# Slot attention with a top-1 switch layer: the second group's outputs finished by slot and scattered to their tokens

## The reference, cut to what matters

```python
x = x + slot_attention(layernorm(x), ctx_1024, ...)          # three GRU steps
t = layernorm(x)
logits = t @ Wg                                               # (4, 512, 8)
gates  = softmax(logits);  expert = argmax(gates)
gate   = gates[expert];    pos = cumsum(onehot(expert)) - 1   # place within the expert
keep   = pos < 64                                             # capacity of an expert, per batch
expert_inputs[e, pos] = t                                     # the kept tokens
y = gelu(expert_inputs @ W1[e]) @ W2[e]                       # (8 experts, 64 slots, 128)
x = x + gate * y[expert, pos]                                 # a dropped token keeps x
```

## Time and profile before

| What | us |
|---|---|
| median of 3 timed runs | 147.28 |
| the profiled execution, its own time | 144.78 |
| its span, first to last instruction | 143.0 |
| so outside the span | 1.8 |
| mean granted TensorE clock in the span | 0.994 |

### The profile page before, as it was taken

The page is one execution under the profiler, slowest core; times in us unless marked ns, Lnnn a source line. Parts: engine busy times, 40 slices in busy tenths (PEclk is TensorE's granted clock), DMA queues, the critical chain, the costliest instruction groups (busy, mean ns, idle before and its releaser), DMA issues.

```text
span 143.0 us, 2755 instructions
## 1 busy us (share of the span) xinstructions
PE 125.9 (88%) x1030; PEld 89.9 (63%) x1030; DVE 95.2 (67%) x305; ACT 80.7 (56%) x156; POOL 33.8 (24%) x54
## 2 busy tenths in 40 slices
PE   6847789999899899899896898699999999889960
PEld 2443466575484575575563764399999899678730
DVE  2895992399699797896998899975781050043851
ACT  1746572586566747847825958963693273044440
POOL 5580922200500501403200052015000187600000
PEclk9999999999999999999999999999999999999997
DMA  3989980000000000000000000000102111102024
GB/s 102 293 221 342 387 298 14 0 0 0 7 0 0 0 0 5 0 2 0 0 5 0 0 0 0 0 5 0 39 5 70 40 37 43 34 5 76 9 66 147
DMA packets 9197, 8.05 MB, mean 56 GB/s; under 512 B 601, under 2 KB 7028, under 8 KB 9184
## 3 DMA queue, kind: packets, MB, share of 16 engines
q1 hardware_dynamic: 8492, 7.28, 15.9%
q0 software_dynamic: 256, 0.40, 1.1%
q10 hardware_dynamic: 436, 0.20, 0.5%
HBM read 6.43 MB, written 1.57 MB: 56 GB/s over the span
## 4 chain that ended last, share of the span: by engine, by line
PE 64%; DVE 16%; ACT 10%; issue 3%; DMA 3%; POOL 2%; ACTq 0%; DVEq 0%
PE ps L1301 11%; PE ps L1287 10%; PE ps L1106 7%; PE ps L1099 6%; PE ps L1133 6%; PE ps L1125 5%; ACT r_b L421 4%; PE ps L1313 3%; PE ps L1207 3%; DMA x_tok<-in_x_dram 3%; PE ps L1170 2%; DVE xn_tok L622 2%; PE ps L1055 2%; PE ps L1082 2%; DVE ps L710 2%
## 5 line engine op out<-in xcount | busy, mean ns | idle before, releaser
L1287 PE MATMUL ps<-h,W_t 128*128 128x128 f32 x128 | 15.9, 279 | 0.0
L1133 PE MATMUL ps<-attn,VW 32*128 32x256 f32 x144 | 12.9, 426 | 3.3 <-DVE ps L710 2.4
L428 ACT ACTIVATE ps<-ps,half_b 128x512 f32<-128x512 f32 x12 | 7.9, 662 | 13.6 <-PE ps L1106 13.6
L1287 PEld LDWEIGHTS ps<-h,W_t 128*128 128x128 f32 x128 | 15.0, 192 | 0.5 <-issue 0.3
L1125 PE MATMUL ps<-h,whhT 128*128 128x256 f32 x48 | 13.5, 403 | 0.0
L1106 PE MATMUL ps<-h,whhT 128*128 128x256 f32 x48 | 13.3, 398 | 0.0
L710 DVE SCALAR_TENSOR_TENSOR ps<-r_b,ps 128x512 f32<-128x512 f32 x12 | 7.8, 693 | 7.7 <-ACT r_b L421 7.7
L345 POOL DMA_INDIRECT y_tok<-y_rows,row_of x8 | 8.5, 1057 | 17.1 <-DMA y_rows<-y_sb 15.0
L1133 PEld LDWEIGHTS ps<-attn,VW 32*128 32x128 f32 x144 | 5.7, 182 | 10.2 <-DVE ps L710 4.8
L1099 PE MATMUL ps<-h,whhT 128*128 128x256 f32 x48 | 11.8, 384 | 0.0
L318 POOL TENSOR_SCALAR mse<-attn 128x8 f32<-128x8 f32 x6 | 1.2, 204 | 44.0 <-DVE attn L645 44.0
(11 more groups left out here) (168 smaller groups left out, 259.5 us busy)
## 6 DMA issues: line engine op xcount, KB each, us to landing
W_t<-in_L_ffn_W_dram SPq DMA_DIRECT2D x1, 2048.0 KB, 10.8
x_tok<-in_x_dram SPq DMA_DIRECT2D x4, 256.0 KB, 4.0
out_dram<-h SPq DMA_DIRECT2D x4, 256.0 KB, 2.3
y_rows<-y_sb SPq DMA_DIRECT2D x4, 128.0 KB, 1.8
n_b<-in_L_xattn_gru_whh_dram SPq DMA_DIRECT2D x1, 192.0 KB, 3.8
n_b<-in_L_xattn_gru_wih_dram SPq DMA_DIRECT2D x1, 192.0 KB, 3.1
y_tok<-y_rows,row_of POOLq DMA_INDIRECT x8
n_b<-in_ctx_dram ACTq DMA_DIRECT2D x1, 64.0 KB, 3.3
```

The lines of the kernel that those rows point to most:

```text
L428: nc.scalar.activation(HV[i], HV[i], ACT.Identity, bias=half_b[:, 2:3]).then_inc(s["hb"], 1)
L1133: last = mm(to[:, hf, :], VW[b][p:p + M, gate * P:(gate + 1) * P], attn[g][p:p + M, :], start=False, stop=True, skip_group_check=True)
L1287: last = mm(hid_bank[e][:, j * BG * CAP:(j + 1) * BG * CAP], W1_t[:, ex_, j * P:(j + 1) * P], rhs, start=True, stop=True)
```

## The change

For group 1 the whole return by matmul goes (`slot_rows`, `rows_out`, `combine_hot`, `y_high`, `y_low`, `combine`, the copies of the sums, `back`, `gated_out`). In its place:

- x of group 1 is kept in `x2_row`, 128 channels, then the gate, then the token's number in `out`: rows of 130 words. SP stores the 128 channels to `out` early, so that dropped tokens are done.
- SP fills an HBM tensor `slot_rows` (1024 rows of 130 words) with a "no token" mark, and POOL writes each token's row to its slot there, 8 indirect DMAs (`file_tokens`), ahead of the 8 fetches of group 0. SP reads it back in slot order (`slot_row`), one DMA a batch.
- Each half of a `down` of group 1 is finished by one DVE instruction (gate times y plus x, `finished_rows`) and written by one indirect DMA of POOL to its tokens in `out` (`send_rows`, 8 of them); rows without a token are out of bounds.
- So the gate of group 1 is needed early: `scale_logits(1)` stands ahead of `place(1)`, `gates(1)` behind it, and `gate_exp(1)` on ACT behind `gelu(1)`, as Tanh with (1 + t) / (1 - t) on DVE instead of Exp. On PE `logits(2)` and `logits(3)` stand ahead of `up(1)`, `positions(1)` ahead of `down(0)`.
- Batch 3's halves of group 1's `down` go to banks 4 and 5. `source_rows` of group 0 move behind the dispatch of group 1.
- PE's preamble has `keep_clock(2)` and `keep_clock(5)` more.

```diff
+            sp.wait_ge(marks, 3)
+            sp.dma_start(slot_rows.ap().rearrange("(k p) d -> p k d", p=P),
+                         no_token[:, :].unsqueeze(1).broadcast_to([P, BG * NP, ROW])).then_inc(cleared, 16)
+            for b in range(BG, B):
+                sp.wait_ge(x2c, b + 1)
+                sp.dma_start(out[b].rearrange("(c p) d -> p c d", p=P),
+                             x2_row[:, (b - BG) * C:(b - BG + 1) * C, 0:D]).then_inc(kept_out, 16)
             for k in range(NP):
                 sp.wait_ge(ysb, k + 1)
                 sp.dma_start(y_rows..., y_sb[:, k, :, :]).then_inc(y_put, 16)
-            for b in range(B):
-                sp.wait_ge(fin, (C, 2 * C, 3 * C, 3 * C + 1)[b])
+            for i in range(BG):
+                sp.wait_ge(tok_put[i], 16 * C)
+                sp.dma_start(slot_row[:, :, i, :], slot_rows...[i]).then_inc(slot_got[i], 16)
+            for b in range(BG):
+                sp.wait_ge(fin, (b + 1) * C)
                 sp.dma_start(out[b]..., res[:, b, :]...).then_inc(out_done, 16)
...
+            def file_tokens(b):
+                for n in range(b * C, (b + 1) * C):
+                    nc.gpsimd.indirect_dma_start(
+                        out=slot_rows.ap(), out_offset=bass.IndirectOffsetOnAxis(ap=row_of[:, n:n + 1], axis=0),
+                        in_=x2_row[:, n - CG, :], in_offset=None,
+                        bounds_check=BG * E * CAP - 1, oob_is_err=False).then_inc(tok_put[b - BG], 16)
+            def send_rows(s, i):
+                k = s - NP
+                pool.wait_ge(rs, BG * k + i + 1)
+                nc.gpsimd.indirect_dma_start(
+                    out=out.rearrange("b n d -> (b n) d"),
+                    out_offset=bass.IndirectOffsetOnAxis(ap=slot_row[:, k, i, TOKEN_AT:ROW].bitcast(u32), axis=0),
+                    in_=y_sb[:, k, i, :], in_offset=None,
+                    bounds_check=B * N - 1, oob_is_err=False).then_inc(rows_out_done, 16)
+            pool.wait_ge(cleared, 16)
+            pool.wait_ge(x2c, B)
+            pool.wait_ge(gt, 2)
+            pool.wait_ge(idx, BG)
+            file_tokens(2)
+            file_tokens(3)
             pool.wait_ge(y_zero, 1)
-            pool.wait_ge(idx, BG)
+            pool.wait_ge(idx, B)
             pool.wait_ge(y_put, 16 * NP)
             fetch_rows(0)
             fetch_rows(1)
+            pool.wait_ge(kept_out, 16 * BG)
+            for s in range(NP, STEPS):
+                send_rows(s, 0)
+                send_rows(s, 1)
...
             gelu(1)
+            gate_exp(1)
             y_out(0)
...
             x2_shift(3)
+            scale_logits(1)
             place(1)
+            source_rows(2)
+            source_rows(3)
+            gates(1)
             dispatch_hot(2)
             x_low(2)
             dispatch_hot(3)
             x_low(3)
+            source_rows(0)
+            source_rows(1)
+            dve.wait_ge(y_put, 16 * NP)
             dve.wait_ge(gt, 1)
+            finished_rows(NP, 0)
+            finished_rows(NP, 1)
             gated_rows(0)
+            finished_rows(NP + 1, 0)
+            finished_rows(NP + 1, 1)
             gated_rows(1)
+            for s in range(NP + 2, STEPS):
+                finished_rows(s, 0)
+                finished_rows(s, 1)
...
             up(0)
             x2_back(3)
-            up(1)
             logits(2)
             logits(3)
+            up(1)
+            positions(1)
             down(0)
-            positions(1)
             up(2)
...
-            slot_rows(2)
-            slot_rows(3)
             pe.wait_ge(xeC, B)
             up(4)
             up(5)
             down(4)
             up(6)
             down(5)
-            combine(4)
             up(7)
             down(6)
-            combine(5)
             down(7)
-            combine(6)
-            combine(7)
-            back(2)
-            back(3)
```

More of the change, by code:

```diff
@@ L463, in gate_exp @@
                 act.wait_ge(gl, g + 1)
-                nc.scalar.activation(lex[:, cs, :], lg[:, cs, :], ACT.Exp).then_inc(lx, 1)
+                if g == 0:
+                    nc.scalar.activation(lex[:, cs, :], lg[:, cs, :], ACT.Exp).then_inc(lx, 1)
+                else:
+                    nc.scalar.activation(lex[:, cs, :], lg[:, cs, :], ACT.Tanh, scale=0.5).then_inc(lx, 1)
             def dispatched_out(b):
@@ L577, in _ @@
             dispatched_out(3)
-            rows_out(2)
-            rows_out(3)
-            gelu(4)
             for s in range(NP, STEPS):
[L582 to L593, removed]
+                gelu(s)
         @block.vector
@@ L829, in gates @@
                 dve.wait_ge(lx, g + 1)
+                if g == 1:
+                    v.tensor_scalar(first[:, cs, :], lex[:, cs, :], -1.0, 1.0, ALU.mult, ALU.add).then_inc(sg, 1)
+                    dve.wait_ge(sg, 1)
+                    v.reciprocal(first[:, cs, :], first[:, cs, :]).then_inc(sg, 1)
+                    dve.wait_ge(sg, 2)
+                    v.scalar_tensor_tensor(out=lex[:, cs, :], in0=lex[:, cs, :], scalar=1.0, in1=first[:, cs, :],
+                                           op0=ALU.add, op1=ALU.mult).then_inc(sg, 1)
+                    dve.wait_ge(sg, 3)
                 v.reduce_sum(lsum[:, cs], lex[:, cs, :], AX).then_inc(ls, 1)
                 dve.wait_ge(ls, g + 1)
-                v.reciprocal(gate[:, cs], lsum[:, cs]).then_inc(gt, 1)
+                v.reciprocal(gate[:, cs] if g == 0 else x2_row[:, :, GATE_AT], lsum[:, cs]).then_inc(gt, 1)
             half_biases()
@@ L895, in _, with source_rows @@
             gates(0)
[L897 to L917, removed]
-                v.tensor_scalar(row_of[:, cs], slot[:, cs], float(i * E * CAP), None, ALU.add).then_inc(idx, 1)
+            def source_rows(b):
+                cs = slice(b * C, (b + 1) * C)
+                dve.wait_ge(pl, 5 * (b // BG + 1))
+                v.tensor_scalar(row_of[:, cs], slot[:, cs], float((b % BG) * E * CAP), None, ALU.add).then_inc(idx, 1)
             def gated_rows(b):
@@ L1017, in _ @@
             tr(bank[0][:, P:2 * P], Wv_t[:, :], ident[:, :]).then_inc(wtr, 1)
+            keep_clock(2)
             pe.wait_ge(m_c, 2)
@@ L1030, in _ @@
             mm(bank[3][:, 256:256 + E], center[:, :], Wg_t[:, :], start=True, stop=True).then_inc(m_p, 1)
+            keep_clock(5)
             norm_T(1)
@@ L1183, in positions @@
                 mm(to, tri[:, :], of, start=False, stop=True, skip_group_check=True).then_inc(posP, 1)
-            def slot_rows(b):
-                g = b // BG
-                pe.wait_ge(pl, 6 * g + 6)
-                pe.wait_ge(x2c, BG)
-                for c in range(C):
-                    last = mm(row_bank[b % BG][:, c * P:(c + 1) * P],
-                              slot_r[:, b * C + c:b * C + c + 1].broadcast_to([P, P]),
-                              ident_r[:, :], start=True, stop=True)
-                last.then_inc(srP, 1)
             def dispatch(b):
@@ L1298, in down @@
                 for i in range(BG):
+                    to = y2_bank if s >= NP and i == 1 else y_bank
                     for j in range(J):
                         for e in range(2):
[L1301 removed]
+                            last = mm(to[s % 2][e * CAP:(e + 1) * CAP, i * D:(i + 1) * D],
                                       hid[s % 2][:, e, j, i * CAP:(i + 1) * CAP], W2_t[:, 2 * k + e, j, :],
                                       start=(j == 0), stop=(j == J - 1))
[L1304 to L1328 removed]
+                    if s >= NP:
+                        last.then_inc(yB, 1)
+                if s < NP:
+                    last.then_inc(yP, 1)
             pe.wait_ge(w1_in, 16)
```

141 lines of the change are left out of this document (48 added, 93 removed).

## The result

The changed kernel takes 148.43 us (median of 6 runs, 147.66 to 149.44), the kernel before 145.45 (6 runs, three of them those of the section above). The ratio is 1.024, interval 1.019 to 1.029: slower. Forecast were 141.6 and the range 138.5 to 145.0. Its profiled execution has a span of 147.7 us where I had 137.3.

What follows compares the result with a forecast made beforehand. PE's chain was taken to bound the kernel before, POOL's queue the changed one: last send 134.04 + 2.3 landing + 0.4 = 136.7, plus 0.6 unplaced waits, 137.3 span; profiled 139.1, median 141.6, range 138.5 to 145.0.

Steps and rivals of the forecast that it cites:

- POOL's queue: POOL's file_tokens, fetches and sends in sequence; claimed to set the end, 2.9 us behind what PE allows.
- a scatter's pitch: Time from one scatter on POOL to the next; taken as the gather's 1.30 us, bounds 1.0 and 2.6.
- PE's new chain: PE's steps after dispatch(3), from up(4) at 115.4; claimed to sum to 15.4 us and end down(7) at 130.8.
- the last send: Eighth indirect DMA of the sends on POOL; claimed to start at 134.04, with its data ready long before.
- Rival 1: POOL's queue: a scatter costs more than a gather, time 158.8 us at pitch 2.6; chance 0.09.
- Rival 2: file_tokens: the dispatch's eight DVE compares hold POOL for 3.8 us, time 144.2; chance 0.09.
- table load: ACT's Tanh between two Gelus: nothing or two loads, delaying PE by at most 0.6 us; taken as nothing.
- the odd stretch: down(5) in the kernel before took 3.71 us where another down takes 1.90; 1.8 us lost, left out of PE's sum.
- rival 3: A PE product is seen late while POOL issues; one hold at the last half gives 143.1 us; chance 0.09.
- the slack of 2.9 us: Amount by which POOL's end was to lie behind what PE allows, covering one mid-kernel hold of 1.8 us.
- POOL's start: Start of file_tokens, after the gates and rows of group 1; claimed at 102.4.
- The 2.5 us: Step from the profiled execution, 139.1, to the median of the timed runs, 141.6, carried over from the kernel before.

Runs made afterwards that it cites:

- a_plain_pool: Changed kernel with the 8 indirect DMAs of file_tokens replaced by 8 plain DMAs issued by POOL; span 138.3 us, repeated on another chip 143.8.
- b_gather15: Kernel before plus 7 close indirect gathers on POOL that nothing reads; span 141.5 us, repeated unchanged on another chip 147.7.
- b_spaced: Kernel before with a POOL memset of about 0.9 us and its wait behind each of the 8 fetches; ratio 1.012 (0.996 to 1.028).

## Why the prediction was wrong

*Read rightly.* POOL's queue as the new bound; a scatter's pitch (1.28, I took 1.30); PE's new chain without holes (131.2 against 130.8) and the last send (134.79 against 134.04), both seen in `a_plain_pool` on the chip without holes. Rival 1 (dear scatters) is refuted. Rival 2 (compares hold POOL) too: the DMAs beside the compares took 1.23, 0.98 and 1.25 us against 0.97, so 0.5 us in the train, not 3.8. Tanh needed no table load: it ran in 0.25 us.

*The step that failed* is in "PE": "I leave out the 1.8 us of the odd stretch here", and with it rival 3. I had seen in the trace of before that PE lost time and its results came late while POOL issued close indirect DMAs, and had noted that the change fills POOL. Then I priced it as one hold, which the slack of 2.9 us covers all or most of, and gave it 0.09. The runs show a hole for nearly every close train: each of the four profiles of the changed kernel has them beside both trains of eight. In the first the train of `file_tokens` cost 5.9 us in `down(2)` and `down(3)`, the lower clock behind it 1.1 in `dispatch` (117.21 to 122.21, 5.0 us, against 3.9 in the kernel before), the fetches 2.0, the first four sends 1.5. That is 10.5 of the 10.9 by which `down(7)` came late, and it is also what lies between its end and that of `down(7)` in `a_plain_pool` (141.73 against 131.19). It is all on PE's path: I had treated POOL's queue and PE's steps as two independent chains, and the first train lies where PE has no slack at all. The fetches then waited for PE, and the sends behind them in the same queue. That the holes come from the close trains is shown, by taking the train away, loosening it, and adding one; that the change would be faster without them is argued, as below.

*Smaller misses.* POOL's start, 103.75 against 102.4, did not matter. From the start of the last send to the end of the span it took 3.5 us (144.24 to 147.7; 134.79 to 138.3 in `a_plain_pool`), I had 2.7, carried over from plain stores. The 2.5 us that I added between the profiled execution and the median of the timed runs did not carry over: here the profiled execution is 1.0 us above the median. The 2.5 us most likely came from runs of the long kind (147.28 and 147.33), whose clock is not on record. `keep_clock` at no cost was right, but I gave its use nothing either, since the one execution I had did not show the fall.

*Not settled.* Why POOL's issue stops PE, and why one chip of those used did not do it. PE's counts arrive late before the hole opens, as if something on their way filled up, but no run tests that. All these times come from runs in which spans and clock were recorded; whether an unrecorded run has the holes is not known. The changed kernel itself never met the chip without holes, so its being faster there is argued from `a_plain_pool`, not shown. Nor was it run with all its trains loosened on a chip with holes.

## What to carry to other kernels

Before you move work to POOL as indirect DMAs, look at what PE does beside the ones that are there: an "issue" gap in PE that ends 1 us after POOL's last one is a price that an added train is likely to ask again. Look also for waits marked "remote" on the engines that read PE's products. If the DMAs must lie beside dense PE work, space them: a memset of 0.3 us and its wait behind each (pitch 2.0 instead of 1.3) gained 1.2% on one chip with holes (0.985 to 0.991) and, with `keep_clock`, 1.7% on another (0.973 to 0.994). On the chip without holes it cost nothing measurable (0.999 to 1.007, with `keep_clock`). This holds as long as the last row still arrives before it is needed. An oddity in the trace that coincides with the engine you are about to fill belongs in the sum, not in the rivals.

## What the runs showed of the hardware

- The same instructions, on two chips, took spans of 141.5 and 147.7 us (`b_gather15`, `b_gather15_2`). `a_plain_pool` was 2.5 us under the shortest undisturbed span of the kernel before on one chip (138.3 against 140.8) and 1.0 over it on the other (143.8 against 142.8): one run each, but with opposite signs.
- Eight plain DMAs issued by POOL took 5.02 us together, against 10.5 for eight indirect ones, and made no hole on the chip where the others did (`a_plain_pool_2`). Their train is over before the 6 us after which the first hole of the changed kernel opens, so whether it is the indirect form or the length of the train that matters is not separated.
- The Trainium skill ("SBUF — State Buffer", "Who interferes with whom") says that PE and ACT never wait on anyone; it speaks of the ports of SBUF. The holes in PE beside POOL's indirect DMAs (5.9 us in the first) lie outside what that sentence covers, or against it; no run here can say which.
- POOL's pacing memsets can hold DVE: in `b_spaced` two compares beside one took 1.86 us, where two took 0.88 in the kernel before. The same section of the skill says that POOL and a DVE instruction in a 2-port mode shut each other out for a whole instruction; this row agrees.
